# First layer of a four-layer graph kernel: the ranking of edges cut into pieces, and half of one product of the second unit moved from VectorE to ScalarE and POOL

## The reference, cut to what matters

```python
g  = exp(coeff * (e[:, :, :, None] - offsets) ** 2)        # 64 Gaussians for each pair of nodes
h  = ssp(einsum('bijg,fg->bijf', g, W1) + b1)              # ssp(x) = softplus(x) - log 2
Wf = einsum('bijf,gf->bijg', h, W2) + b2
rf = einsum('bjd,fd->bjf', r, Wa)
Wf = Wf * Am                                               # Am = A[:, :, :, None]
y  = einsum('bjf,bijf->bif', rf, Wf * Am)                  # so the square of A enters
y  = ssp(einsum('bif,df->bid', y, Wd1) + bd1)
y  = einsum('bid,ed->bie', y, Wd2) + bd2
```

## Time and profile before

| | us |
|---|---|
| median of 3 runs | 1319.08 |
| lowest and highest | 1318.16, 1323.06 |
| the profiled execution | 1328.99 |
| its span on the core | 1327.2 |
| DVE busy in the span | 918.7 |
| ACT busy in the span | 929.1 |
| PE busy in the span | 1120.4 |
| POOL busy in the span | 723.0 |

### The profile page before, as it was taken

How to read it: one execution, slowest core, us unless ns; L and a number is a source line. 1 busy time by engine, 2 the same in 40 slices (tenths; PEclk the granted TensorE clock), 3 DMA queues, 4 the chain that set the end, 5 groups by cost and what they waited for, 6 DMA issues and landing times. The chain is left out here.

```text
span 1327.2 us, 28584 instructions
## 1 busy us (share of the span) xinstructions
PE 1120.4 (84%) x6028; PEld 770.1 (58%) x6028; DVE 918.7 (69%) x3889; ACT 929.1 (70%) x2685; POOL 723.0 (54%) x1258
## 2 busy tenths in 40 slices
PE   2588888888888888888874789999789999999974
PEld 1254554544554554444543577777568888887873
DVE  3588988989999988888853798998413333333357
ACT  2488888878888888888761688888535555555566
POOL 6276777766777777676664899998300000000036
PEclk9999999999999999999985899999789999999978
DMA  1788999878789799889920000000000000000013
GB/s 48 151 186 170 174 197 165 179 183 179 172 195 175 176 185 166 178 169 189 174 80 27 17 17 25 17 25 17 1 5 17 13 17 17 13 17 17 12 33 96
DMA packets 130489, 129.31 MB, mean 97 GB/s; under 512 B 61123, under 2 KB 111711, under 8 KB 130401
## 3 DMA queue, kind: packets, MB, share of 16 engines
q1 hardware_dynamic: 128676, 127.19, 46.0%
q10 hardware_dynamic: 1725, 1.13, 0.3%
HBM read 123.05 MB, written 5.21 MB: 97 GB/s over the span
## 5 line engine op out<-in xcount | busy, mean ns | idle before, releaser
L803 PE MATMUL wf<-hid,w2t 128*128 128x384 f32 x512 | 201.0, 516 | 61.2 <-DVE msg L979 61.2
L1810 POOL MEMSET r_minus_half<- 128x4 f32 x1 | 0.1, 102 | 307.7 <-POOLq L1652 307.7
L803 PEld LDWEIGHTS wf<-hid,w2t 128*128 128x128 f32 x512 | 87.7, 191 | 136.1 <-issue 102.3
L585 POOL TENSOR_TENSOR sum<-msg 128x384 f32<-128x384 f32 (+1 forms) x128 | 150.4, 1175 | 29.0 <-DVE msg L979 28.4
L979 DVE SCALAR_TENSOR_TENSOR msg<-wf,b2c,rv 128x768 f32<-128x768 f32 x128 | 129.8, 1014 | 10.0 <-PE wf L803 10.0
L696 ACT ACTIVATE expd<-zb,safe_b,reached 128x768 f32<-128x768 f32 x128 | 125.0, 977 | 2.6 <-PE zb L789 2.4
L1758 DVE SCALAR_TENSOR_TENSOR r_new<-r_gates 128x64 f32<-128x64 f32 x128 | 28.8, 225 | 141.4 <-ACT r_gates L1732 141.4
L952 DVE TENSOR_TENSOR rv<-rg,sq_bc 128x768 f32<-128x768 f32 x128 | 121.4, 948 | 2.7 <-PE rg L832 2.7
L701 ACT ACTIVATE hid<-expd 128x768 f32<-128x768 f32 x128 | 108.0, 844 | 17.7
L788 PE MATMUL zb<-gauss,w1t 64*128 64x384 f32 x256 | 117.8, 541 | 0.0
L789 PE MATMUL zb<-gauss,w1t 64*128 64x384 f32 x256 | 117.8, 541 | 0.0
(11 more groups left out here) (302 smaller groups left out, 3335.8 us busy)
## 6 DMA issues: line engine op xcount, KB each, us to landing
sq_bc<-edge_sq SPq DMA_DIRECT2D x64, 768.0 KB, 7.1
val_bc<-edge_val SPq DMA_DIRECT2D x128, 192.0 KB, 5.7
idx_bc<-edge_idx SPq DMA_DIRECT2D x64, 384.0 KB, 6.7
adj_w<-in_adj_rows SPq DMA_DIRECT2D x64, 64.0 KB, 6.4
xt_w<-in_x_cols SPq DMA_DIRECT2D x64, 64.0 KB, 6.1
xin<-in_x_rows SPq DMA_DIRECT2D x32, 128.0 KB, 6.5
m_adj_g<-in_adj_rows SPq DMA_DIRECT2D x16, 256.0 KB, 2.8
adjt<-in_adj_t SPq DMA_DIRECT2D x32, 128.0 KB, 2.1
```

The costliest lines, as they stand in the source:

```text
L585: pool.tensor_tensor(sum1[:, 0:wide, :], m[:, 0:wide, :], m[:, wide:2 * wide, :], ALU.add)\
L803: last = pe.matmul(wf[:, half, 0:HALF], w2t[:, :], hid[:, q, half * HALF:(half + 1) * HALF], start=True, stop=True)
```

## The change

Everything is in the first layer.

- **The product of the second unit.** DVE computes only the first half (384 columns) of `rv` for second units. For the other half, ACT copies `rg`'s second bank to a new SBUF tile `rg_copy`, at the head of its second step, and POOL multiplies that with the squares into `rv`, behind its test for negatives and ahead of the second unit's sums. `msg` of the second unit waits for the new semaphore `half_scaled`, as do the next load of squares on SP and the next `rg_copy`. PE's next gather into `rg` waits for `rg_copied`.
- **The ranking in pieces.** `rank_edges` becomes five functions: `first_ranks` (a MAX8) ahead of the first unit's `rv`, `second_ranks` behind it, `third_ranks` behind `t_h`, `count_overflow` behind the first unit's `msg`, and `convert_indices` in the second step ahead of `rv`. `place_overflow` keeps the copy of the start, now ahead of `xres`, and the rest becomes `cover_slots`.
- **PE.** The matmul of `p_start` moves from before to behind the second unit's `wf`.

Of `rank_edges` and `place_overflow` the bodies stay as they were, cut at the new functions' heads.

```diff
--- before.py
+++ after.py
+    rg_copy = sb("rg_copy", [P, HALF])
...
@@ -430,6 +431,8 @@
                 q = u.mod(UNIT_BUFS, d)
                 after(sp, "rv_ready", u, d + 1 - UNIT_BUFS, u0)
+                alone(sp)
+                after(sp, "half_scaled", g, dg - 2, 0)
                 alone(sp)
                 sp.dma_start(sq_bc[:, q:q + 2, :], edge_sq[bass.ds(g.at(dg), 1), :, :, :]
                              .rearrange("a k i r -> a k (i r)").broadcast_to((P, 2, UNIT))).then_inc(sq_in[q], 16)
...
@@ -573,6 +576,13 @@
                         w(pool, "rfmid_ready", g.at(1) + g0 + 1)
                         pool.tensor_tensor(rf_lo[:, g.mod(2, 1), :], rf_r1[:, :], rf_mid[:, g.mod(2, 1), :],
                                            ALU.subtract).then_inc(s["rflo_ready"], 1)
+                    if not dense and k_in == 1 and g.has(0):
+
+                        w(pool, "rg_copied", g.at() + 1)
+                        pool.wait_ge(sq_in[loaded(u, 0)], unit_count(u, 0, 16))
+                        pool.sem_inc(k["held"]["Pool"], 1)
+                        pool.tensor_tensor(rv[:, u.mod(2), HALF:UNIT], rg_copy[:, :], sq_bc[:, u.mod(UNIT_BUFS), HALF:UNIT],
+                                           ALU.mult).then_inc(s["half_scaled"], 1)
                     if u.has(0):
                         q = u.mod(2)
@@ -665,6 +675,10 @@
                 for i in range(per_pair):
                     u, g = unit(pair, i), graph(pair, i)
                     k_in = i % per_graph
+                    if not dense and k_in == 1 and g.has(0):
+                        w(act, "rg_ready", u.at() + 1)
+                        after(act, "half_scaled", g, -1, 0)
+                        act.activation(rg_copy[:, :], rg[:, 1, 0:HALF], ACT.Copy).then_inc(s["rg_copied"], 1)
                     if not dense and k_in == 1 and g.has(-1):
                         w(act, "over_u_p", g.at(-1) + 1)
                         after(act, "u_ready", g, -2, 0)
@@ -788,13 +802,6 @@
                         pe.matmul(zb[:, 0, 0:HALF], w1t[0:NG, :], gauss[0:NG, qn, :], start=True, stop=True)
                         pe.matmul(zb[:, 1, 0:HALF], w1t[NG:P, :], gauss[NG:P, qn, :], start=True, stop=True)\
                             .then_inc(s["z_ready"], 1)
-                    if not dense and k_in == 1 and g.has(4):
-
-                        w(pe, "cnt", g.at(4) + 1)
-                        if g.has(1):
-                            w(pe, "rfhi_ready", g.at(1) + 1)
-                        pe.matmul(p_start, before[:, :], over_cnt[:, bass.ds(g.at(4), 1)], start=True, stop=True)\
-                            .then_inc(s["start_ready"], 1)
                     if u.has(0):
                         w(pe, "hid_ready", u.at() + u0 + 1)
@@ -803,6 +810,13 @@
                             last = pe.matmul(wf[:, half, 0:HALF], w2t[:, :], hid[:, q, half * HALF:(half + 1) * HALF],
                                              start=True, stop=True)
                         last.then_inc(s["wf_ready"], 1)
+                    if not dense and k_in == 1 and g.has(4):
+
+                        w(pe, "cnt", g.at(4) + 1)
+                        if g.has(1):
+                            w(pe, "rfhi_ready", g.at(1) + 1)
+                        pe.matmul(p_start, before[:, :], over_cnt[:, bass.ds(g.at(4), 1)], start=True, stop=True)\
+                            .then_inc(s["start_ready"], 1)
                     if k_in == 1 and g.has(-1):
                         gl = g.mod(2, -1)
@@ -824,6 +838,8 @@
                         gn, kn = Steps(g.pair, (i + 1) // per_graph, 2, ng), (i + 1) % per_graph
                         w(pe, "pick_ready", u.at(1) + u0 + 1)
                         after(pe, "rv_ready", u, 0, u0)
+                        if not dense and k_in == 1 and g.has(0):
+                            w(pe, "rg_copied", g.at() + 1)
                         if kn == 0:
                             w(pe, "rflo_ready", gn.at() + g0 + 1)
                         for half in range(2):
...
-            def rank_edges(g):
+            def first_ranks(g):
...
+                dve.max(found[:, q, 0:8], adj_w[:, q, :]).then_inc(s["top1"], 1)
+
+            def second_ranks(g):
...
+            def third_ranks(g):
...
+            def count_overflow(g):
...
+            def convert_indices(g):
...
+            def cover_slots(g):
...
                                           ALU.is_equal).then_inc(s["pick_ready"], 1)
+                    if not dense and k_in == 0 and g.has(4):
+                        first_ranks(g)
+                    if not dense and k_in == 1 and g.has(4):
+                        convert_indices(g)
                     if u.has(0):
...
-                        dve.tensor_tensor(halves(rv[:, u.mod(2), :]), rg[:, :, 0:HALF], halves(sq_bc[:, u.mod(UNIT_BUFS), :]),
+                        wide = 1 if not dense and k_in == 1 else 2
+                        dve.tensor_tensor(halves(rv[:, u.mod(2), :])[:, 0:wide, :], rg[:, 0:wide, 0:HALF],
+                                          halves(sq_bc[:, u.mod(UNIT_BUFS), :])[:, 0:wide, :],
                                           ALU.mult).then_inc(s["rv_ready"], 1)
+                    if not dense and k_in == 0 and g.has(4):
+                        second_ranks(g)
                     if k_in == 0 and g.has(-2):
...
                     if not dense and k_in == 0 and g.has(4):
-                        rank_edges(g)
+                        third_ranks(g)
+                    if not dense and k_in == 1 and g.has(4):
+                        place_overflow(g)
...
-                        place_overflow(g)
+                        cover_slots(g)
...
                         w(dve, "rv_ready", u.at() + u0 + 1)
+                        if not dense and k_in == 1:
+                            w(dve, "half_scaled", g.at() + 1)
...
+                    if not dense and k_in == 0 and g.has(4):
+                        count_overflow(g)
                     if not dense and k_in == 1 and g.has(4):
                         finish_edges(g)
```

More of the change, by code:

```diff
@@ L876, in rank_edges @@
                 alone(dve)
+                dve.max(found[:, q, 0:8], adj_w[:, q, :]).then_inc(s["top1"], 1)
+            def second_ranks(g):
+                q, n = g.mod(2, 4), g.at(4) + 1
                 adj, ranked = adj_w[:, q, :], found[:, q, :]
-                dve.max(ranked[:, 0:8], adj).then_inc(s["top1"], 1)
                 w(dve, "top1", n)
@@ L885, in rank_edges @@
                 dve.max(ranked[:, 8:16], adj_r1[:, :]).then_inc(s["top2"], 1)
+            def third_ranks(g):
+                n, ranked = g.at(4) + 1, found[:, g.mod(2, 4), :]
                 w(dve, "top2", n)
@@ L907, in place_overflow @@
                 dve.tensor_copy(start, p_start).then_inc(s["start_copied"], 1)
+            def cover_slots(g):
+                n = g.at(4) + 1
+                start = found[:, g.mod(2, 4), 2 * RANKS:2 * RANKS + 1]
                 w(dve, "start_copied", n)
```

5 lines of the change are left out of this document (3 added, 2 removed).

## The result

The changed kernel takes 1433.89 us (median of 4 runs, 1430.73 to 1434.3) beside 1318.62 us for the kernel before on the same chip. The ratio is 1.0859, with a 95% interval of 1.0822 to 1.0897: 8.6% slower. The profiled execution took 1434.26 us, with a span of 1432.4.

A forecast was written before the change was run, and what follows sets the result against it. DVE was taken to set the pace at 10.02 us a graph; a new loop through POOL's product takes 11.37, +80 us over 59 graphs, +8 at the end: 1319.08 + 88 = 1407 us, range 1380 to 1442.

The forecast's parts named there:

- The loop: First layer, second `msg` to the next through POOL's product: 11.37 us a graph against 10.02, 80 us for 59 graphs.
- the stretch from the second `msg` over `pick` to `rv`: First three links on DVE: 1.37 us to `pick`, 0.49 to the next instruction, 0.20 for the MAX8 ahead of `rv`.
- The last four graphs: End of the first layer: 9.70 us a graph against 7.95, about 8 us more with the last half graph.
- The product: POOL's 128x384 multiplication ahead of the second `msg`: 1.00 us, bounds 0.95 and 1.41.
- Half of `rv` off DVE: nothing: Saves DVE about 0.42 us a graph between first and second `msg`, where it will wait for POOL: worth nothing.
- Ranking in pieces: nothing: DVE's split ranking frees the first `msg` earlier, but that `msg` is not on the loop: worth nothing.
- The dependent waits: In DVE's ranking, 0.24 us lost at each of four places, 0.96 a graph; most saved, but worth nothing.
- The wait for the start: DVE waits 0.6 us for `p_start` behind the second unit's `wf`, covered by 2.6 us of waiting for POOL.
- The signs: Profile after: second `msg` waits 2 to 3 us, 60 times; 6.7 us from first `msg`; DVE's first-layer share below 80%.
- The first rival: POOL keeps up and its own list bounds: 9.2 us a graph with handovers, -48 us, so 1271; chance 4%.
- The second: POOL splits `rf` early and begins the sums at the first `msg`: 10.6 us a graph, 1360 us; chance 6%.
- The third: Clock dips each graph and PE's links double: 12.7 us a graph, about +168 us, 1487; chance 7%.

## Why the prediction was right

The forecast was 1407 us, within 1380 to 1442. Measured are 1433.9. The mechanism, its place and its sign were right; the size was 27 us short.

That 1433.9 lies inside the range owes something to luck. Upwards, 24 of the 29 us of the prediction's own range came from a product of 1.41 us (0.41 in 59 graphs), and the product took 1.00. Without that bound the range would have ended near 1412, or 1418 with the widening. The terms that did move were others, as follows.

**The loop.** Forecast 11.37 us a graph, measured 11.82 and 11.54 by turns, 11.68 in the mean. Link by link, forecast and measured in the graph shown above:

| link | forecast | measured |
|---|---|---|
| second `msg` to `pick` | 1.37 | 1.81 (1.38 in the next graph) |
| `pick` to MAX8 | 0.49 | 0.43 (0.74 in the next) |
| MAX8 to `rv` | 0.20 | 0.26 |
| `rv` to the gather on PE | 1.10 | 1.11 |
| gather to the matmul of `rf`, to ACT, to `rf_hi`, to POOL | 2.20 | 2.24 |
| splitting of `rf` | 1.38 | 1.51 (1.56 in the next) |
| first unit's sums | 2.45 | 2.41 |
| negatives | 1.03 | 1.02 |
| product and handover | 1.15 | 1.03 |
| sum | 11.37 | 11.82 (11.54 in the next) |

The term that was mis-sized is the stretch from the second `msg` over `pick` to `rv`, the first three links. I took 1.37 and 0.49 from single places of the trace before. In every second graph DVE's list turns around its loop there, with 0.34 us of issue ahead of `pick`. The trace before had that too, in the very next graph, 1.80 us behind the second `msg` at 412.51, under another name:

```profile
414.31 0.63 DVE L943 TENSOR_SCALAR pick<-idx_bc,iota_col 128x768 bf16<-128x768 bf16 x1 [0.35 <-PE rg L832]
```

In the other graphs `pick` lasts 0.82 us and not 0.42, beside POOL's sums, which now start right behind the second `msg`. The stretch was forecast at 2.06 us and took 2.50 or 2.32, so 0.35 more in the mean; the other links together give back 0.04. The 0.31 us that are left make 18 us in 59 graphs, and with 0.6 us less than forecast in the last four graphs that is the 105.3 - 88 = 17 us by which the first layer's loss was missed. The rest of the 27 us is that the profiled execution before lay 10 us above its median, and the one after did not (1434.26 against 1433.89); I had carried that difference over, and the 10.02 us a graph that I compared with were too many for the median.

**The last four graphs.** Forecast +8 us, measured 42.5 against 35.1 us, +7.4.

**The product.** Forecast 1.00 us, by the slope between 128 and 512 dense columns; measured 0.996 in the mean of 64. The bound from the strided sums (1.41) was far off, and the choice of the row with dense operands was right. The 1.41 was no price of strides alone either: such a sum takes 1.29 us when no `pick` of DVE runs beside its start (last section).

**Half of `rv` off DVE: nothing.** Confirmed. It is 0.545 us for 384 columns against 0.944 for 768, so 0.40 saved, all of it in front of the wait for POOL. With the wait mended, the kernels with and without the product part are equal if the start matmul is in front (0.980 and 0.979), and the product part costs 0.6% if it is behind.

**Ranking in pieces: nothing.** This step was wrong in its reason; its number was right only for the kernel with both parts. I held that the first `msg` was off the loop, and it is, because of the pieces. Without them it would have been on it, and the changed kernel 0.41 us a graph slower. I should have worked out the loop with the old order as well.

**The dependent waits.** Forecast 0.96 us a graph on DVE, of which 0.6 would be lost again to the start matmul. The ranking part alone gives a ratio of 0.9848, which is 20 us or 0.31 us a graph, close to the 0.36 that is left of 0.96. (The spacings, 10.01 and 9.38, would say 0.63, but both profiled executions were off their medians, the one before by 10 us upwards and this one by 4 downwards.) DVE waits 13.9 us in 32 graphs for the start, 0.43 each. The rule of the Trainium skill (VectorE: DVE Perf Modes, Rules for kernel authors), by which the number of chained instructions counts and not the semaphores between them, would have given no gain, since the pieces have the same instructions; the measured ratio of 0.9848 decides for the row. No run has the pieces with the waits alone changed, so how much of the gain is the waits and how much is the earlier first `msg` is not shown.

**The wait for the start.** Forecast 0.6 us, measured 0.64. It was covered by the wait for POOL, as forecast: 2.6 us of cover, measured 2.55.

**The signs.** The second `msg` waits 64 times, 2.55 us in the mean; from a first `msg` to the second it is 6.7 us; DVE's share in the first layer is 69%. From a second `msg` to the next first it is 4.87 and 5.07 by turns, forecast 4.7. POOL's wait for `rf_hi` was to stay near 1 us and was 1.65 in the mean (42.8 us in 26 graphs).

**The first rival** (POOL keeps up) put 9.2 us a graph on a kernel in which the product does not hold up the second `msg`. The run with the product ahead of the sums made that kernel: 9.55. There DVE waited for the start (26.0 us in 31 graphs) and, less, for the adjacency load (10.4), which none of my rivals named; POOL itself still waited for `rf_hi`, 19.8 us in 31 graphs, so its list was not the bound. **The second** (the splitting of `rf` comes early, 1360 us) did not occur either: POOL waited for `rf_hi` in each of the 26 graphs between 200 and 500 us. **The third** (the clock) did not occur: PE's waits for `msg` stayed at about 1.4 us, as the prediction held, and the clock at 1.00. The doubled product shows it with waits of 2.1 to 2.4 us.

## What to carry to other kernels

Before work is moved to an engine with slack, ask where in that engine's list it will stand and what the instructions ahead of it wait for. Here POOL was idle for a quarter of the time, and the same kernel was 8.6% slower with the product behind the sums and 0.9% faster with it ahead of them. Slack is only worth something where the list can be at the product early enough; add up the chain from the last use to the next, around the whole iteration, and compare it with the bound of today.

When a change has two parts, price the loop with each part alone. The ranking in pieces alone, at 0.979, is as good as anything with the product part, and needs less.

A profiled execution is one execution. Before its spacings are subtracted from those of another kernel, compare each with the median of its runs; here that alone was 10 us.

## What the runs showed of the hardware

- With the product twice, PE idled 2.1 to 2.4 us ahead of `wf` in most graphs of 13.17 us, and the granted clock was 0.88 to 0.89 in every stretch of the first layer; 1.3 to 1.4 us in each graph of 11.68 left it at 1.00. The one does not follow from the other graph by graph: in 4 of 27 graphs the gather right behind such an idle stretch still ran at the full level (so at 264.86, idle 2.28, gather 0.32 us), where the graph before had idled only 0.8 to 1.0.
- `pick`, a bf16 TENSOR_SCALAR of 768 columns on DVE, took 389 ns at best and 817 ns at most in the changed kernel, the long ones where one of POOL's sums had started some 0.3 us earlier (418.04 to 418.86, L595 from 417.76 to 418.64). The Trainium skill, page SBUF — State Buffer, section Terms, says that DVE and GpSimd share a pair of ports which one of them holds for a whole instruction. The trace agrees in direction for this form of instruction, and it goes both ways: where `pick` starts first, it is POOL's sum that takes longer (next point). `rv` and `msg` varied by some 3%.
- On POOL a dense product of 384 columns took 1.00 us. The sum of 384 strided columns took 1.28 to 1.30 us in the 63 cases of the changed kernel in which no `pick` overlapped it, and 1.40 to 1.43 us in the 58 cases of the kernel before in which a `pick` had started just before it; the other 6 there took 1.29.
